# First layer of a two-layer decoder kernel: in odd slots the linear half's value products first, then the context's value products (moved in from the even slots before), then the context's scores

## The reference, cut to what matters

```
x = x + linear_attention(layernorm(x))            # 16 heads of 16, causal, elu(q)+1 and elu(k)+1
x = x + softmax(q k^T / 4 + mask) v  over the context, projected
x = x + experts(layernorm(x))                     # 16 experts, top 2, capacity 640
```

## Time and profile before

| | |
|---|---|
| median of 3 runs | 1672.96 us (1669.79 to 1673.18) |
| traced execution, device time | 1675.36 us |
| its span | 1673.6 us |
| PE busy | 1536.0 us, 92% of the span |
| DVE busy | 979.0 us, 58% |
| ACT busy | 842.2 us, 50% |
| POOL busy | 468.4 us, 28% |
| mean granted TensorE clock | 0.968 of full speed |

### The profile page before, as it was taken

How to read it: one execution, slowest core, us unless ns; L and a number is a source line. 1 busy time by engine, 2 the same in 40 slices (tenths; PEclk the granted TensorE clock), 3 DMA queues, 4 the chain that set the end, 5 groups by cost and what they waited for, 6 DMA issues and landing times. The chain is left out here.

```text
span 1673.6 us, 27432 instructions
## 1 busy us (share of the span) xinstructions
PE 1536.0 (92%) x10279; PEld 1083.3 (65%) x10279; DVE 979.0 (58%) x2296; ACT 842.2 (50%) x1849; POOL 468.4 (28%) x592
## 2 busy tenths in 40 slices
PE   8999999998987899999999899999999989996299
PEld 5676767766755777787777466666666654442288
DVE  3665766767766435222222567766664568777883
ACT  4446555555555422211212565666656533597980
POOL 4223234253234410000002665555542300032100
PEclk9999999999998999999999999999999889998599
DMA  3440111011151154334424211110100000000031
GB/s 115 156 156 18 47 30 44 30 47 44 34 165 39 61 164 137 125 113 126 153 87 136 70 39 52 43 34 27 39 14 14 1 25 1 0 1 15 24 99 65
DMA packets 100929, 108.32 MB, mean 65 GB/s; under 512 B 25410, under 2 KB 89804, under 8 KB 100800
## 3 DMA queue, kind: packets, MB, share of 16 engines
q1 hardware_dynamic: 94656, 90.01, 17.3%
q0 software_dynamic: 6144, 16.57, 3.1%
HBM read 64.77 MB, written 42.01 MB: 64 GB/s over the span
## 5 line engine op out<-in xcount | busy, mean ns | idle before, releaser
L1795 POOL TENSOR_SCALAR c_pr<-c_pr,c_rsum 128x256 f32<-128x256 f32 x256 | 128.2, 518 | 190.2 <-DVE c_rsum L2211 189.8
L2089 ACT ACTIVATE c_pr<-bank,c_nmax 128x256 f32<-128x256 f32 x256 | 118.0, 473 | 119.9 <-DVE c_nmax L2206 119.8
L1526 ACT ACTIVATE b_G<-bank 128x320 f32<-128x320 f32 x128 | 56.0, 437 | 210.8 <-PE bank L1475 210.8
L1475 PE MATMUL bank<-b_XT,shared 128*128 128x320 f32 x512 | 154.6, 437 | 0.0
L2206 DVE TENSOR_REDUCE c_nmax<-bank 128x2 f32<-128x512 f32 x128 | 82.4, 685 | 108.6 <-PE bank L1854 108.5
L1489 PE MATMUL bank<-shared,b_G 128*128 128x256 f32 x640 | 142.2, 379 | 0.0
L1489 PEld LDWEIGHTS bank<-shared,b_G 128*128 128x128 f32 x640 | 120.9, 190 | 17.8
L1072 DVE TENSOR_TENSOR hT_all<-bank,a_causal 128x512 f32<-128x512 f32 x128 | 79.4, 682 | 67.5 <-PE bank L563 67.5
L498 POOL TENSOR_TENSOR a_L<-a_L,a_Lm 128x1232 f32<-128x1232 f32 x32 | 72.0, 2249 | 149.5 <-DVE a_Lm L1087 149.5
L1475 PEld LDWEIGHTS bank<-b_XT,shared 128*128 128x128 f32 x512 | 92.5, 193 | 27.6 <-issue 1.2
L1545 DVE COPY b_Y<-bank 128x256 f32<-128x256 f32 x80 | 33.9, 424 | 120.3 <-PE bank L1489 120.1
(11 more groups left out here) (376 smaller groups left out, 3400.2 us busy)
## 6 DMA issues: line engine op xcount, KB each, us to landing
shared<-L_ffn_w SPq DMA_DIRECT2D x32, 512.0 KB, 6.0
t_slots_in<-a_h SPq DMA_DIRECT2D x20, 512.0 KB, 7.5
shared<-t_slots_in SPq DMA_DIRECT2D x15, 640.0 KB, 7.3
t_slots_out<-b_Y SPq DMA_DIRECT2D x15, 640.0 KB, 4.1
hT_all<-x SPq DMA_DIRECT2D x8, 512.0 KB, 4.0
a_xr<-x SPq DMA_DIRECT2D x8, 512.0 KB, 3.9
t_x_a<-a_x SPq DMA_DIRECT2D x8, 512.0 KB, 2.9
shared<-t_x_a SPq DMA_DIRECT2D x8, 512.0 KB, 4.3
```

The costliest lines, as they stand in the source:

```text
L1475: t = p.matmul(P[2 + n % 2][:, 0:HC], w1[e % 3][:, u, 128 * f:128 * f + 128], XT[e % 2][:, u, HC * m:HC * m + HC], start=(u == 0), stop=(u ...
L1795: p.tensor_scalar(pr[k][:, e, u, :], pr[k][:, e, u, :], rsum[k][:, e, u:u + 1], 1.0, ALU.mult, ALU.mult).then_inc(q.pr_ready, 1)
L2089: a.activation(pr[t % 2][:, e, u, :], P[e][:, S * u:S * u + S], ACT.Exp, bias=nmax[t % 2][:, e, u:u + 1], accum_out=sums[t % 2][:, e, u:u ...
```

## The change

The work is the same, instruction for instruction; its order changes.

- PE: in odd slots `x_scores` moves behind `values`. `x_values(g - 3, 1)` moves from the end of slot 2 to slot 3, and `x_values(g - 2, 0)` from slot 6 to slot 7, in both between `values` and `x_scores`. In slot 3 the turns of the third norm (`turn2a/b`) come ahead of `xtok2/3`.
- ACT: `keep_x_values` moves from slot 2 to 3 and from 6 to 7, behind `keep_values` and ahead of `by_key`, and so behind `exponents` of the slot it left.
- `UNITS`: the rotation of banks follows.
- DVE and POOL keep their order.

```diff
-                 2: (("proj1", -1), ("xproj0", -3), ("xval1a", -3), ("xval1b", -3), ("pkt", 1)),
-                 3: (("val1", 0),) + tuple((n, -2) for n in turned(0)) + (("xtok2", -3), ("xtok3", -3), ("turn2a", -4), ("turn2b", -4), ("xv", -1)),
+                 2: (("proj1", -1), ("xproj0", -3), ("pkt", 1)),
+                 3: (("val1", 0), ("xval1a", -3), ("xval1b", -3)) + tuple((n, -2) for n in turned(0)) + (("turn2a", -4), ("turn2b", -4), ("xtok2", -3), ("xtok3", -3), ("xv", -1)),
...
-                 6: (("proj0", 0), ("turn1a", -1), ("turn1b", -1), ("xval0a", -2), ("xval0b", -2), ("turn0a", 2), ("turn0b", 2),
+                 6: (("proj0", 0), ("turn1a", -1), ("turn1b", -1), ("turn0a", 2), ("turn0b", 2),
                      ("rank", -4), ("state0", 1), ("state1", 1)),
-                 7: (("val3", 0),) + tuple((n, -2) for n in turned(2)) + (("xq0", -1),)}
+                 7: (("val3", 0), ("xval0a", -2), ("xval0b", -2)) + tuple((n, -2) for n in turned(2)) + (("xq0", -1),)}
...
                     if s % 2 == 0 and now:
                         scores(g, s // 2)
+                    if s % 2 and now:
+                        values(g, s // 2)
+                    if s == 3 and back3:
+                        x_values(g - 3, 1)
+                    if s == 7 and back2:
+                        x_values(g - 2, 0)
                     if s % 2 and back2:
                         x_scores(g - 2, s // 2)
-                    if s % 2 and now:
-                        values(g, s // 2)
...
                     if s == 2:
-                        if back3:
-                            keep_x_values(g - 3, 1)
...
                     if s == 3:
+                        if back3:
+                            keep_x_values(g - 3, 1)
                         if back2:
                             by_key(g - 2, 0)
...
                     if s == 6:
-                        if back2:
-                            keep_x_values(g - 2, 0)
...
                     if s == 7:
                         if back2:
+                            keep_x_values(g - 2, 0)
                             by_key(g - 2, 2)
```

More of the change, by code:

```diff
@@ L810, in _ @@
                             project("xproj0", g - 3, axT, xwo, 0)
-                            x_values(g - 3, 1)
                         if ahead1:
@@ L816, in _ @@
                             x_turn(g - 2, 0)
+                        if back4:
+                            turn_norm(2, g - 4, h2[(g - 4) % 2])
                         if back3:
@@ L821, in _ @@
                             to_tokens("xtok3", g - 3, oxT, 3)
-                        if back4:
-                            turn_norm(2, g - 4, h2[(g - 4) % 2])
                         if back1:
@@ L860, in _ @@
                             turn_norm(1, g - 1, h1)
-                        if back2:
-                            x_values(g - 2, 0)
                         if ahead2:
```

## The result

The changed kernel has a median of 1680.95 us over 6 runs (1676.02 to 1683.07), the kernel before one of 1673.07 us over 6: ratio 1.0048, 95% interval 1.0029 to 1.0066. It is slower, by some 4 to 8 us (medians apart by 7.9 us, and by 4.2 on the other occasion); forecast were 5.3.

A forecast was written before the change was run, and what follows sets the result against it. The prediction took PE, busy 92% of the span and in the first layer a queue with hardly a hole, as the bound. Its terms, 6.0 - 3.1 + 0.85 + 1.7 - 0.2 = +5.3 us, gave 1678.3 us, range 1670.5 to 1683.

The forecast's parts named there:

- Slot 7 to slot 0: Periods 4 to 7: later context scores delay VectorE's masked and the division freeing xtok0's bank; +6.0 us over four.
- Slot 1: Slot 0 to 1, periods 2 to 7: value products fill the 0.89 us wait for query columns; -3.1 us together.
- Slots 3 to 5: Periods 2 to 7: later scores delay VectorE and ScalarE's norm, mostly absorbed except in period 3; +0.85 us.
- the changes between tile shapes: Moved products beside column-tiled ones: forecast saw at most 0.1 us in a change and counted nothing in its sum.
- tile changes cost time: Rival: fewer changes between column, row and full-array tiles save PE 5.6 us, giving 1672.7 us; chance 0.15.
- PE's value and score products take less time in their new order: Sign named in advance that would show the forecast to be wrong; no size given.
- The drain: Periods 8 to 11: ranks wait ahead of value products, clock falls in period 9, +1.7; earlier exponent in period 8, -0.2.
- The clock at the new waits: Rival: clock also falls behind tok2's waits in periods 5 and 6; +3.3 us on top, 1681.6; chance 0.20.
- The sum: All terms of the first layer together: +5.3 us, giving a predicted 1678.3 us.
- The rival that VectorE's delay is hidden: Slots 0 to 5: xtok0 is free when it was, so the removed waits are gained; -7.5 us, 1665.5; chance 0.12.

The follow-up runs named there:

- the other occasion: The changed kernel run again unchanged, 12 runs, against the kernel before: ratio 1.0031.
- e3: The changed kernel with the router's 14 small VectorE steps moved in periods 4 to 7 from slot 7 to the end of the next slot 0: ratio 0.9916 to the kernel before.
- e5: The changed kernel with the context's scores ahead of the linear values again, the rest as changed: ratio 0.9957 to the kernel before.
- e7: The kernel before with the router's small VectorE steps moved from slot 7 to behind the divisions of the next slot 0: ratio 0.9946 to the kernel before.
- e4: The kernel before with the linear values ahead of the context's scores in slot 1 alone: ratio 0.9970 to the kernel before.
- e2: The kernel before with only the linear values ahead of the context's scores in odd slots; context's value products and banks unmoved: ratio 1.0052 to the kernel before.
- e6: The changed kernel with the old order in slots 6 and 7 of periods 8 to 11, value products ahead of the ranks: ratio 0.9990 to the kernel before.
- e9: The changed kernel with the third norm's turns in slot 3 back behind xtok2/3: ratio 1.0121 to the kernel before.

## Why the prediction was right, point by point

- *Slot 7 to slot 0.* Right in mechanism and size. Forecast: `masked` 1.6 us later against slot 6. It starts 9.79 us after slot 6's linear scores before (323.59 to 333.38) and 11.26 after (322.09 to 333.35): +1.5. The wait of L649 is 2.05 us, forecast 1.9; the turn's wait for `proj0`'s bank 0.98, forecast 0.9. e3, e5 and e7 show that this queue of VectorE carries the cost. With slot 1 of the same periods the term is +6.0 instead of +5.0, since slot 1 gives back nothing there.
- *Slot 1.* Right in mechanism: no L578 wait in periods 2 to 7, a wait of 0.69 us of L690 in its place from period 4 on, forecast 0.7. In periods 2 and 3 the gain was 1.16 us each instead of 0.89. Of the rest, 0.10 is the next point but one. Another 0.15 is an overlap that a wait takes away: L615 passes on after 1.83 us where nothing is waited for (345.57 to 347.40), while a product that waits starts behind the end of its row of 1.98 us. So each wait that goes is worth some 0.15 us more than its number. From period 4 on the gain was 0.0, forecast 0.3 each (period 4 here, periods 4 to 6 in e4).
- *Slots 3 to 5.* In period 3 slots 4 and 5 are 1.4 us longer, forecast 1.35 (a wait of 1.50 us of L656), and slots 2 and 3 are 0.5 shorter, which was not forecast: +0.9 together. For periods 4 to 6 I had forecast 0, since ScalarE's chain would end when it did; measured are -0.7, -0.7 and -1.3. Of each, 0.5 is the next point. The rest is 0.2 in periods 4 and 5 and 0.8 in period 6, where nearly the whole wait of L680 that went was gained. In period 5 the wait of L690 for `a_oT` in slot 5 shrank from 0.63 to 0.17 us: ScalarE's chain ended a little earlier than before, not when it did.
- *The step that was mis-sized most: the changes between tile shapes*, which the prediction set to nothing. The rows show about 0.1 us each in two places. The full-array state products L591 go from start to start of the next in 0.54 us when no row-tiled scores stand ahead (329.13 to 329.67) against 0.64 before (332.90 to 333.54 in the trace before; the row of L591 in rows 2 has 0.71 for its four, the one of after 0.61). And column tiles followed by column tiles take 0.89 us (L597 to L704, 329.67 to 330.56), against 1.01 followed by row tiles. The experiments separate the term: slots 2 and 3 of period 3, which hold no wait in any of these traces, are 0.48 us shorter in the changed kernel, 0.19 in e2 (the linear values moved) and 0.29 in e5 (the context's values moved). With these 0.48 us in periods 3 to 7, and 0.22 from slot 6 to slot 0 of periods 2 to 7 (measured in 2 and 3), I estimate 3.7 us of TensorE time less, part of which ends in waits for VectorE and ScalarE. So the rival "tile changes cost time" was half right. I gave 5.6 us for it. Both pairs of rows that I compared are themselves changes of shape, column to row tiles and row tiles to the full array, so that they could not show what a change costs. The Trainium skill's sentence that a change of mode drains TensorE ("TensorEngine Tiling (Array Packing)", key properties) fits these 0.1 us; it gives no figure. The prediction had named "PE's value and score products take less time in their new order" as a sign that it is wrong; that sign came, beside the longer wait of L649.
- *The drain.* Right in mechanism, too small: I took a fall of the clock in period 9 alone. It fell in period 8 too, behind a wait of 1.95 us that I had not counted since no row of L751 in the trace before shows a wait there. In return the fall behind the 4.31 us of L690 in the trace before did not come. Measured +3.0 (and 4.6 against e6), forecast +1.5. The drains of other kernels differ by up to 5 us with one and the same order, so that this number is in part chance.
- *The clock at the new waits.* It stayed up behind the 2.05 us of L649 in both traces of the changed kernel. In e2 it fell behind one of the same two waits. Behind the waits of 2.19 us in e2 and e9 it fell three times in nine. The rival that priced these falls, +3.3 us, was thus possible in any execution. The remaining 1 to 4 us of the medians go with a lower mean clock of the longer executions; behind which waits it fell there stays open.
- *The sum* was right by errors that cancel, and so by luck: -4 us not seen in slots 2 to 6 and from slot 6 to 0 of periods 2 and 3, +1.0 in slots 6 to 1 and +1.5 in the drain. Up to `xq1` of period 8 the forecast was +3.75 us and the traces show +0.6. The rival that VectorE's delay is hidden is refuted: VectorE had no hole from `masked` to the division, in either trace.

## What to carry to other kernels

Where an in-order engine has a long queue between two things that the busiest engine gives and takes, the time at which its first input is made sets the time at which the last comes back. Where that queue has no hole, as here, moving work ahead of such a producer costs its whole length at the far end; moving it behind the producer (e5), or moving steps of the queue that nobody waits for behind the point that is waited for (e3, e7), gains it. A change made of several parts should be priced part by part: here the place of the scores cost 6.0 us up to `xq1` of period 8 and hid a gain of 5.4 us from the other parts.

Two equal end times do not show equal courses: e3 and e7 end the first layer at the same 591.3 us, with 4.0 us between them in the steady state and 4.0 the other way in the drain. Cut a trace into stretches, and compare those that the edit doesn't touch first: they tell how much is chance.

When a pipeline drains, an order that suited its steady state can put a waiting instruction in front of work that had covered the wait. Here the clock fell behind both of these waits of 2 to 3 us, and the value products behind them took 1.7 and 1.05 us longer.

## What the runs showed of the hardware

- Equal waits are not followed by equal clocks: L680 waited 2.19 us nine times in e2 and e9, and took 3.50, 1.95, 1.95, 1.95 us behind it in e2 and 3.24, 3.64, 1.95, 1.95, 1.95 in e9. A wait of 3.57 us was followed by a row of 3.55 us in the kernel before, and one of 3.58 us at the same place by 1.98 us in e4; one of 1.95 us in the changed kernel's drain by a granted clock of 0.51.
- The small VectorE step with two operands in SBUF (L1182, 128x8) took 2.16 to 2.17 us where GpSimd's subtraction ran beside it, in the kernel before and in the changed one: moving both moves the stall, too. Where the step stood apart from the subtraction (e3, e7) it took 0.17 us.
- A group of 32 column-tiled products (L597) passes on to the next after 0.89 us if that is column-tiled too, and after 1.01 to 1.02 us if it is row-tiled or takes the full array.
- A stretch of the same instructions up to period 1 took 60.3 to 62.3 us in the twelve traces, with nothing changed in it.
